# Two-layer attention on one core: row-tiled masks, maxima carried in idle contraction rows, and a re-merged order of steps

## What is computed

```
L0:  Q,K,V = relu(x Wq'+bq), relu(ctx[:, :112] Wk'+bk), relu(... Wv'+bv)   16 heads of 16
     a = softmax(mask(Q K'/4)) ; x = layer_norm(a V + x)     mask: causal, and keys whose features sum to 0
L1:  q,k,v = ln1(x) Wqkv ; a = softmax(mask(q k'/16)) ; r = x + (a v) Wp + bp    mask: causal, padding
     q2 = ln2(r) Wq2 ; k2,v2 = ln2(ctx) Wkv                                375 keys, no mask
     r = r + (softmax(q2 k2'/16) v2) Wp2 + bp2
     out = r + relu(ln3(x) W1 + b1) W2 + b2
```

## Time and profile before

| | |
|---|---|
| median of three runs | 367.59 us |
| profiled execution | 367.8 us, span 366.1 us |
| TensorE, VectorE, ScalarE, GpSimd busy | 348.3, 224.6, 170.9, 52.2 us |
| TensorE's share of the chain that ended last | 76% |
| moved by DMA | 14.12 MB |

### The profile page before, as it was taken

The page is one execution under the profiler, slowest core; times in us unless marked ns, Lnnn a source line. Parts: engine busy times, 40 slices in busy tenths (PEclk is TensorE's granted clock), DMA queues, the critical chain, the costliest instruction groups (busy, mean ns, idle before and its releaser), DMA issues.

```text
span 366.1 us, 9692 instructions
## 1 busy us (share of the span) xinstructions
PE 348.3 (95%) x4144; PEld 262.9 (72%) x4144; DVE 224.6 (61%) x563; ACT 170.9 (47%) x299; POOL 52.2 (14%) x67
## 2 busy tenths in 40 slices
PE   8988999999999999999999999999999999999996
PEld 4656788777965678876876776766987768675674
DVE  4789998436668746567945758556944464264412
ACT  2267652650664255673444062763453643614350
POOL 2023331041022010122100041130100031000000
PEclk9999999999999999999999999999999999999999
DMA  7759202000000002000000200000000000000000
GB/s 200 218 192 376 69 23 92 2 2 0 27 0 2 2 7 81 27 14 15 3 2 8 79 2 14 2 2 14 1 4 0 2 2 2 15 2 13 4 2 25
DMA packets 5300, 14.12 MB, mean 39 GB/s; under 512 B 689, under 2 KB 2982, under 8 KB 5002
## 3 DMA queue, kind: packets, MB, share of 16 engines
q1 hardware_dynamic: 4970, 13.42, 11.1%
q10 hardware_dynamic: 288, 0.09, 0.1%
HBM read 12.59 MB, written 0.92 MB: 37 GB/s over the span
## 4 chain that ended last, share of the span: by engine, by line
PE 76%; DVE 13%; DMA 5%; ACT 2%; issue 2%; SPq 1%; POOL 0%; DVEq 0%
PE ring L501 35%; PE ring L743 8%; PE acc L647 8%; PE ring L757 5%; PE ring L622 5%; DVE negmax L1031 4%; PE ring L602 4%; PE ring L596 3%; DMA xh<-in_keys 3%; PE ring L634 2%; DVE negmax L1010 2%; PE ring L666 2%; PE ring L614 2%; DMA w_qk<-in_w_qk 1%; PE ring L708 1%
## 5 line engine op out<-in xcount | busy, mean ns | idle before, releaser
L1031 DVE TENSOR_REDUCE negmax<-ring 112x2 f32<-112x750 f32 x64 | 57.0, 936 | 23.7 <-PE ring L743 23.0
L856 ACT ACTIVATE exps<-ring 125x896 f32<-125x896 f32 x48 | 41.4, 914 | 39.5 <-PE ring L757 39.2
L1248 POOL TENSOR_SCALAR_AFFINE_SELECT exps<-exps 112x896 f32<-112x896 f32 x32 | 30.8, 987 | 118.9 <-ACT exps L856 118.9
L1010 DVE TENSOR_REDUCE negmax<-ring 112x8 f32<-112x896 f32 x32 | 33.4, 1085 | 22.1 <-PE ring L602 22.0
L743 PE MATMUL ring<-k,q 32*112 32x376 f32 x256 | 38.5, 518 | 1.2 <-ACT exps L856 0.5
L647 PE MATMUL acc<-exps,v 125*17 125x112 f32 (+1 forms) x1280 | 38.9, 261 | 0.2
L647 PEld LDWEIGHTS acc<-exps,v 125*17 125x17 f32 (+1 forms) x1280 | 28.1, 97 | 12.9 <-issue 10.3
L856 ACT ACTIVATE exps<-ring,pad 112x896 f32<-112x896 f32 x32 | 30.5, 1004 | 10.7 <-PE ring L634 10.6
L501 PE MATMUL ring<-w_b,h 128*112 128x256 f32 x128 | 29.3, 382 | 0.0
L501 PEld LDWEIGHTS ring<-w_b,h 128*112 128x112 f32 x128 | 22.1, 177 | 5.8 <-issue 1.1
L501 PE MATMUL ring<-n,w_b 128*128 128x224 f32 x128 | 25.7, 357 | 0.2
(11 more groups left out here) (139 smaller groups left out, 547.2 us busy)
## 6 DMA issues: line engine op xcount, KB each, us to landing
c_nat<-in_ctx SPq DMA_DIRECT2D x4, 750.0 KB
w_b<-in_w_b SPq DMA_DIRECT2D x1, 2304.0 KB, 13.4
xk_t<-in_xk_t SPq DMA_DIRECT2D x8, 224.0 KB, 4.6
w_a<-in_w_a SPq DMA_DIRECT2D x1, 1280.0 KB, 6.0
xh<-in_keys SPq DMA_DIRECT2D x4, 224.0 KB, 4.1
x_nat<-in_x SPq DMA_DIRECT2D x4, 224.0 KB, 3.3
out<-x SPq DMA_DIRECT2D x8, 112.0 KB, 1.8
rows_sb<-in_row SPq DMA_DIRECT2D x1, 560.0 KB, 7.8
```

The source lines that it names most:

```text
L856: return nc.scalar.activation(exps[0:k, EXP_AT[job], :, :], o[0:k, :, 0:4 * T], ACT.Exp, bias=bias)
L1010: v_max[b].step(nc.vector.tensor_reduce(negmax[0][:, slot(g, b), 2 * m_:2 * m_ + 2, :], o[0:T, :, 0:4 * T].rearrange("p r (j t) -> p r j t ...
L1031: x_max[b].step(nc.vector.tensor_reduce(negmax[1][:, b, 2 * m_:2 * m_ + 2, i], o[0:T, :, 0:S], AX.X, ALU.max, negate=True), g, 2 * i + m_ + 1)
L1248: p_masked[b].step(nc.gpsimd.affine_select(e, e, [[0, 8], [1, T]], ALU.is_ge, 0.0, base=0, channel_multiplier=-1), g, k)
```

## The change

1. **Masks on row tiles.** The mask is laid out so that key row 32j + i of block j lies on partition i of every strip. A mask is now written by 16 bf16 matmuls of 32 (the last four of 16) contraction rows: four blocks times four strips, 128 (64) columns each. The L0 mask needs the zero-sum keys on all strips: a new step **rep** (TensorE: four matmuls of two columns, in each group) spreads them, and VectorE makes the two masks from PSUM (128 x 448 each). The L1 mask is made by GpSimd from the given padding, also 128 x 448 each. VectorE's 16 small mask operations go.
2. **Maxima in idle rows.** Keys are now stored twice too (`kf`, `k2`): copy e holds one head of the strip, and zero in the other head's 16 rows save a one at row c. VectorE writes the maxima straight into a zeroed fp32 tile; M is one fp32 transpose; a new step **Q** on VectorE (two operations, `less_maximum`) adds the transposed minus-maxima into the idle rows of the query copies. X is then 16 fp32 products of 112 columns, which subtract the maximum by themselves. `minus_max`, the fp32r split (L1014, L1016), `sel`, `maxrows` and ScalarE's copies (L849, L852) go. ScalarE writes keys in four instead of two (L0), four instead of one (L1) and four instead of two (k2, per sequence) operations.
3. **Start.** The flag's branch now stands ahead of the k0 projection, and in the first rep TensorE runs four more 512-column matmuls on zeros. The mask constants grow from 73.5 KB to 276 KB.
4. **New merge.** `MIX` is another string, of 350 steps instead of 322 (rep and Q are steps).

The core of the diff:

```diff
 def c_steps(g, b):
-    return [("S", g, 0, b), ("M", g, 0, b), ("X", g, 0, b), ("V", g, 0, b), ("O", g, 0, b), ("dev", g, b), ("norm", g, b),
+    return [("S", g, 0, b), ("M", g, 0, b), ("Q", g, 0, b), ("X", g, 0, b), ("V", g, 0, b), ("O", g, 0, b), ("dev", g, b), ("norm", g, b),
...
-MIX = ("ALALNNCANDEECDCNPICWNCWDPJEWJICPDDICPJDN
+MIX = ("ALLNANNCADECDECDNCDNPNWCICPJENDIJIJDWIPC
...
+            def keys_replicated(g):
+                o = claim(pe, ("rep", g))
+                if g == 0:
+                    pe.wait_ge(prep_dve, PREP_DVE)
+                    keep_busy(4, acc[0][:, :, :].rearrange("p s t -> p (s t)"))
+                    pe.wait_ge(mask_const_loaded, 16)
+                pe.wait_ge(*v_mask.done(g))
+                for j in range(J):
+                    m = nc.tensor.matmul(o[:, 0, j * G:(j + 1) * G], spread_j[:, j, :], pad0b[:, slot(g, 0):slot(g, G)], ...)
...
-                for r in range(R):
-                    nc.tensor.matmul(bank(r)[0:T, 0:4 * T], add_mask[:, l, slot(g, b), :], ident_b[:, :].unsqueeze(1).to_broadcast([T, 4, T]), ...)
+                for j in range(J):
+                    n = min(32, T - 32 * j)
+                    for r in range(R):
+                        rows = slice(32 * r, 32 * r + n)
+                        nc.tensor.matmul(bank(r)[0:T, 0:4 * T].rearrange("p (h t) -> p h t", h=4)[:, :, 32 * j:32 * j + n], add_mask[rows, l, slot(g, b), j, :],
+                                         ident_j[rows, 0:n].unsqueeze(1).to_broadcast([n, 4, n]), ...)
...
-                for e in range(2):
-                    m = nc.tensor.matmul(o[:, 0, e * T:(e + 1) * T], spread[i][:, 128 * e:128 * e + 128], ident_r[:, :], ...)
+                end(nc.tensor.transpose(o[:, 0, 0:T], spread[i][:, :], ident[0:T, 0:T]))
...
-            def minus_max(bank, i, k):
+            def shifted(bank, k, keys, queries):
                 for c in range(C):
-                    for r in range(R):
-                        nc.tensor.matmul(bank(r)[0:k, 2 * c * T:2 * (c + 1) * T], sel[rows, c:c + 1].to_broadcast([32, k]), maxrows[i][rows, :], ...)
+                    for e in range(2):
+                        for r in range(R):
+                            rows, j = slice(32 * r, 32 * r + 32), 2 * c + e
+                            m = nc.tensor.matmul(bank(r)[0:k, j * T:(j + 1) * T], keys(rows, c, e), queries(rows, c, e), ...)
...
+            def less_maximum(signal_, g, k, job, q, b):
+                o = is_filled(dve, job)[:, 0, 0:T].unsqueeze(1).to_broadcast([128, C, T])
+                for e in range(2):
+                    signal_.step(nc.vector.scalar_tensor_tensor(q[:, :, b, e, :], o, vec[:, EO + 1 - e:EO + 2 - e], q[:, :, b, e, :], ALU.mult, ALU.add), g, 2 * k + e - 1)
```

More of the change, by code:

```diff
@@ L29 @@
 NE = 6
+J = 4
 class Signal:
@@ L624, in self_max_rows @@
             def self_max_rows(g, l, b):
-                max_rows(("M", g, l, b), v_spread[b].at(g, 2 * l + 2))
+                max_rows(("M", g, l, b), slot(g, b), v_max[b].at(g, 4) if l else v_seen[b].done(g))
             def self_shifted(g, l, b):
                 bank = quad(("X", g, l, b))
-                pe.wait_ge(*a_m[b].at(g, l + 1))
-                minus_max(bank, slot(g, b), T)
-                for c in range(C):
-                    for r in range(R):
-                        rows = slice(32 * r, 32 * r + 32)
-                        m = nc.tensor.matmul(bank(r)[0:T, 2 * c * T:2 * (c + 1) * T], kf[g % 2][rows, c, b, :],
-                                             qf[g % 2][rows, c, b, :, :].rearrange("p e t -> p (e t)"), start=False, stop=True, skip_group_check=True)
-                        if c == C - 1 and r % 2:
-                            end(m)
+                pe.wait_ge(*v_less[b].at(g, 2 * l + 2))
@@ L742, in cross_scores @@
                     rows = slice(32 * r, 32 * r + 32)
-                    m = nc.tensor.matmul(bank(r)[0:T, 0:SP], q2[g % 2][rows, c, b, e, :], k2[g % 2][rows, b, c, :], start=True, stop=True)
+                    m = nc.tensor.matmul(bank(r)[0:T, 0:SP], q2[g % 2][rows, c, b, e, :], k2[g % 2][rows, b, c, e, :], start=True, stop=True)
                     if r % 2:
@@ L1220, in _ @@
             dve.wait_ge(prep_dve, PREP_DVE)
-            run({"rows": rows_summed, "flag": flag, "general": general, "f": add_hidden, "split": weights_lo, "keys": keys, "masks": masks, "late": late_masks, "v0": values0, "S": self_maxima, "M": self_spread, "O": self_out, "dev": deviation0, "norm": norm1,
+            run({"rows": rows_summed, "flag": flag, "general": general, "f": add_hidden, "split": weights_lo, "keys": keys, "rep": masks0, "masks": masks, "late": late_masks, "v0": values0, "S": self_maxima, "M": seen, "Q": self_less, "O": self_out, "dev": deviation0, "norm": norm1,
                  "v1": values1, "proj": residual1, "norm2": norm2,
-                 "stats": context_statistics, "cnorm": context_shift, "cT": context_lo, "v2": values2, "cS": cross_maxima, "cM": cross_spread,
+                 "stats": context_statistics, "cnorm": context_shift, "cT": context_lo, "v2": values2, "cS": cross_maxima, "cQ": cross_less,
                  "cO": lambda g, b: out_normed(("cO", g, b), x_o[b], 1, g, b, b), "y": result})
@@ L1248, in masked, with masks1 @@
                     p_masked[b].step(nc.gpsimd.affine_select(e, e, [[0, 8], [1, T]], ALU.is_ge, 0.0, base=0, channel_multiplier=-1), g, k)
+            def masks1(g):
+                if g == 0:
+                    pool.wait_ge(mask_const_loaded, 16)
+                    pool.wait_ge(pads_made, 1)
+                for b in range(G):
+                    if g > 1:
+                        pool.wait_ge(*v_max[b].done(g - 2))
+                    p_mask1.step(nc.gpsimd.tensor_tensor(add_mask[:, 1, slot(g, b), :, :], causal_j, pad1_j[:, :, G * g + b].unsqueeze(2).to_broadcast([128, J, T]), ALU.add), g, b + 1)
             def deviations2(g):
```

236 lines of the change are left out of this document (112 added, 124 removed).

## The result

The changed kernel took 372.38 us (median of 9 runs, 369.84 to 372.95) against 367.64 us (9 runs, 366.7 to 372.64) of the kernel before: a ratio of 1.0103 with a 95% interval of 1.0071 to 1.0134. The forecast was 354.0 us with a range of 346 to 361: wrong in sign, by 18 us. The profiled execution took 372.7 us (span 370.9), to be held against 367.8 (366.1).

What follows compares the result with a forecast made beforehand. The prediction took TensorE's work to bound the kernel: 16.8 us saved behind 60 us, less 1.5 for idle time and 1.5 for the start, is 13.8 us off 367.8, so 354 us, with a range of 346 to 361.

Steps and rivals of the forecast that it cites:

- the sum: Whole kernel: 16.8 us of TensorE work saved behind 60 us, less 1.5 for idle time and 1.5 for the start: 13.8 us.
- Part 6: Start: first scores at about 13.4 us instead of 11.32; the stage to 60 us ends 1.5 us later (bounds 0 and 4).
- Part 1: X steps on TensorE without `minus_max`: 0.99 us each instead of 1.25, a gain of 0.26 us x 40 = 10.4 us.
- the S products are the same tiling: Mask step on TensorE: ground for pricing 16 pairs at 31 ns, 0.50 us against 0.85, a gain of 5.6 us.
- Part 5: Other engines: VectorE gains net 13 us (67% of the span), ScalarE about 9 us (51%), GpSimd eight masks; hidden behind TensorE.
- first rival: Freed TensorE time turns into waits for VectorE, half of the 16.8 us going so: 361 us, chance 0.14.
- GpSimd gets eight masks at 14% load; hidden: GpSimd's L1 masks: the added work was to cost the kernel no time.
- The way from maxima to X stays about as long: Chain of maxima, transpose, Q, X against maxima, split, M, copy, X: about the same length as before.
- second rival: More saved than counted: X worth 5.0 us more, masks at the column floor 3.2 more, start breaking even: 347 us, chance 0.18.
- an X step over 1.1 us: Sign named in advance that the prices were wrong; X was forecast at 0.95 to 1.05 us from start to next start.
- idle time over 26 us: Sign named in advance for waits: TensorE busy as forecast, about 329 us, with VectorE's maxima or Q named as releasers.

Runs made afterwards that it cites:

- k0_first: The changed kernel with the k0 projection of group 0 moved back ahead of the flag's branch: 369.98 us, 1.0058 to the kernel before.
- fewer_masks: The kernel before with each bank's mask matmul 112 columns long instead of 448, leaving out the mask for three of four heads' maxima: 363.53 us, 0.9877.
- q_small: The changed kernel with Q's VectorE operations on one column instead of 112, so the maximum is subtracted for the first query only: 367.98 us, 0.9999.
- pool_ts: `start_mended` with GpSimd's masks made by four one-input operations instead of one two-input addition: 367.34 us, 0.9977 to the kernel before.
- start_mended: `k0_first` with rep of group 1 moved ahead of the context statistics of group 0: 369.53 us, 1.0051 to the kernel before.
- x_old: `pool_ts` without Q: M, X, k2 and kf as in the kernel before, still in the new order, no zero matmuls: 394.5 us, 1.0699.
- masks_only: The kernel before, in its own order, with only the row-tiled masks and rep right behind keys: 373.65 us, 1.0176.
- masks_homes_ts: `masks_only` with the PSUM banks of the kernel before and GpSimd's masks made by four one-input operations: 369.47 us, 1.0035.

## Why the prediction was wrong

Against the sum, both made of the profiled executions and TensorE's timelines, 18.6 us are missing: 5.6 at the start, 9.3 in saved work, 3.7 in idle time. How they split into start and saved work is an estimate, by the steps that lie on either side of 60 us.

- **Start, forecast 1.5 us late, found 7.1** (TensorE's work that the kernel before has done by 60 us and the changed one has not): 5.6 us. The step that failed is Part 6, "the same set of steps (both X, the scores of group 1) should be done at nearly the same time as before". The first scores came at 15.25 us instead of 13.4: the flag's matmul was 0.6 us later (8.92 against 8.35), TensorE waited 1.16 us for the flag's value, and the clock fell to the 1.2 GHz level, which the prediction had no term for. A mean clock of 0.90 between 12 and 60 us is worth 4.8 us at most, less as TensorE was idle for part of it; `k0_first`, faster at 0.86, shows that it does not decide alone. The prediction's own row said that two engines were near their limit here.
- **Work saved behind 60 us, forecast 16.8, found 7.5**: 9.3 us. The failed term is Part 1, 0.26 x 40: the 36 X steps there saved 0.5 us instead of 9.4. Its two prices were of different kinds. 1.25 us was what an X step took before with its usual delays (50.5 / 40 = 1.26); 0.99 us was the price of S products that waited for nobody. At their cheapest the X steps went from 1.15 to 0.98 us (self) and from 1.17 to 1.07 (cross, 125 weight columns, for which I had no row), which is 5.1 us for all 40. The rest went into delays: many steps take 1.2 to 1.7 us at full clock, and some stop after four records, where the second pair of banks begins, for ScalarE's exponentials or VectorE. That the new form meets more of these waits is read from the trace; why it does is not shown. M gained 0.14 us a step, not 0.2 (2.6 us instead of 4.0). Masks went the other way (7.0 us instead of 3.9): 0.25 us at best, near the column floor of 0.21, against the forecast of 0.50. My ground, "the S products are the same tiling", was wrong: one-pass bf16 pairs cost 16 ns, not 31. About 2.3 us were lost in other steps, over 1 us of it by the half clock of 280.8 to 284.2 us, which the prediction had no term for either.
- **Idle time behind 60 us, forecast +1.5, found +5.2**: 3.7 us. The failed step is Part 5 with the first rival's counter-argument, "2.6% idle time in the middle stage, so the order gives TensorE other work in nearly every such wait". `fewer_masks` shows about half of freed time turning into waits, `q_small` that VectorE's 12 us are worth 4.4. Low idle time showed that the order fitted those durations, not that there was slack. Part 5 also put too little on the other engines: VectorE gained 19.9 us instead of 13, ScalarE 14.0 instead of 9. That rival was the right mechanism, at 0.14 and 361 us too weak, as it left out start, clock and X.
- **"GpSimd gets eight masks at 14% load; hidden"** was wrong by contention, not by load: 2.2 us (`pool_ts` against `start_mended`).
- "The way from maxima to X stays about as long" left out that M now comes earlier after its scores, and that the new order counts on it: with the old form in its place TensorE waits 13.3 us there (`x_old`), while the old form in its own order waits 0.7. So `x_old` prices the mismatch of code and order, not the worth of the new form.

The second rival's sum was off by itself: 354 less 5.0, 3.2 and 1.5 is 344.3 us, not 346. Of the signs named in advance, an X step over 1.1 us came, and so did idle time over 26 us (30.0) with maxima among the releasers, though TensorE was busy for 340.9 us and not for 329.

What stays open: how the loss splits between banks and GpSimd in `masks_only`; whether the setting `dynamic_dma_scratch_size=1024`, which every kernel with strip masks has and the kernel before has not, costs or gives anything; why X stops after four records in some steps and not in others; and what another layout of the order would give the new code. The best right form found, `pool_ts`, equals the kernel before (0.9977, interval 0.9945 to 1.0008); none that computes everything is faster for certain.

## What to carry to other kernels

Where a hand-laid order keeps an engine at 95%, its idle time tells nothing of slack: here about half of what was freed arrived, and in `masks_homes_ts` none. Swap old code into the new order, and new code into the old, before crediting either. Compare a floor with a floor: a price taken from a step that never waits for its banks says little of one that does. Let no small new step (here rep) stand ahead of queued work on the fullest engine before its input is there.

## What the hardware showed unexpectedly

- 16 one-pass bf16 pairs of weight load and matmul (32 or 16 rows x 112 weights, 128 or 64 columns) over four strips pass in 0.25 us, 16 ns a pair, while f32 products of 112 columns on the same strips take 31 ns a pair.
- A GpSimd addition of 128x448 bf16 with two inputs takes 939 ns (L1259, median of eight), and VectorE operations beside it grow: two-element ones from 0.18 to 0.93 us, a 112x256 addition from 418 to 2576 ns.
- The granted clock fell to 0.50 inside the kernel after idle stretches of TensorE that were each under 1 us (0.68, 0.99 and 0.36 us between 22 and 27 us; 0.80 and 0.59 us between 273 and 279 us). At that level k0 took 2.49 us instead of 1.77 (at 10.26 us, behind 2.33 and 1.16 us of idle time).
- Other PSUM banks for the same instructions in the same order cost 0.9% (1.0086, 1.0055 to 1.0116).
